# Attention with paired exponentials, bursts of six score pairs, a fold left out and weight loads moved

## The reference, cut to what matters

```python
qkv = jnp.einsum('bsd,de->bse', x, Wqkv)
q, k, v = jnp.split(qkv, 3, axis=-1)
q = _layernorm_scale_only(q, q_ln_scale)
k = _layernorm_scale_only(k, k_ln_scale)
...
scores = jnp.einsum('bshd,bthd->bhst', q / jnp.sqrt(jnp.float32(HEAD_DIM)), k)
scores = jnp.where(causal, NEG_INF, scores)
attn = jax.nn.softmax(scores, axis=-1)
ctx = jnp.einsum('bhst,bthd->bshd', attn, v)
out = jnp.einsum('bsd,de->bse', ctx.reshape(B, S, D_MODEL), out_W)
```

## Time and profile before

| | us |
|---|---|
| median of three runs | 2298.71 |
| lowest and highest | 2298.39, 2300.82 |
| profiled execution, its own time | 2299.94 |
| its span in the profile | 2298.2 |

### The profile page before, as it was taken

How to read it: one execution, slowest core, us unless ns; L and a number is a source line. 1 busy time by engine, 2 the same in 40 slices (tenths; PEclk the granted TensorE clock), 3 DMA queues, 4 the chain that set the end, 5 groups by cost and what they waited for, 6 DMA issues and landing times.

```text
span 2298.2 us, 35041 instructions
## 1 busy us (share of the span) xinstructions
PE 2245.0 (98%) x12270; PEld 1427.9 (62%) x12270; DVE 1698.9 (74%) x1749; ACT 1366.4 (59%) x2821; POOL 302.8 (13%) x366
## 2 busy tenths in 40 slices
PE   9999999999899998999989999899999999999997
PEld 7888854444344443444434444488888888888886
DVE  7777768889798897988979989845655555565554
ACT  4444479999899998999989999611111111101111
POOL 2111122111221112221122211100000000000001
PEclk9999989999999999999999999999999999999999
DMA  7768896657656577556675555831102111110100
GB/s 261 260 239 283 275 247 143 147 132 164 143 135 146 131 158 151 130 141 136 148 158 133 138 120 134 247 108 37 56 19 74 38 37 40 35 55 19 37 19 20
DMA packets 139410, 292.93 MB, mean 127 GB/s; under 512 B 15944, under 2 KB 41032, under 8 KB 127568
## 3 DMA queue, kind: packets, MB, share of 16 engines
q1 hardware_dynamic: 125840, 194.72, 29.6%
q0 software_dynamic: 13104, 95.43, 18.6%
q10 hardware_dynamic: 288, 0.52, 0.1%
HBM read 122.83 MB, written 72.37 MB: 85 GB/s over the span
## 4 chain that ended last, share of the span: by engine, by line
PE 74%; DMA 4%; ACT 4%; DVE 1%; SPq 1%; issue 1%; POOL 0%; DVEq 0%; ACTq 0%; POOLq 0%
PE slot L1555 20%; PE ctx_acc L1145 18%; PE score L1130 18%; PE y L1566 10%; PE slot L1480 3%; ACT probs L1211 3%; PE score_spare L1130 3%; DMA side_odd<-total 2%; DMA side_odd<-probs 1%; PE score L877 1%; DMA queries<-shift 1%; SPq L76 1%; PE slot L1523 1%; POOL probs L1057 0%; PE y L1480 0%
## 5 line engine op out<-in xcount | busy, mean ns | idle before, releaser
L1211 ACT ACTIVATE probs<-score 128x512 f32<-128x512 f32 (+3 forms) x1977 | 987.3, 694 | 69.9 <-DVE total L1273 25.4
L1268 DVE TENSOR_TENSOR total<-total,probs 128x2048 f32<-128x2048 f32 (+3 forms) x440 | 932.2, 2119 | 107.3 <-ACT probs L1211 52.3
L1130 PE MATMUL score<-queries,keys 98*128 98x512 f32 (+3 forms) x1973 | 572.8, 402 | 26.7 <-ACT probs L1211 24.0
L1130 PEld LDWEIGHTS score<-queries,keys 98*128 98x128 f32 x1973 | 346.2, 190 | 366.8 <-ACT probs L1211 287.0
L1631 ACT ACTIVATE hidden<-slot,gate_scale_sb 128x512 f32<-128x512 f32 x128 | 88.4, 690 | 631.6 <-PE slot L1555 628.2
L1145 PE MATMUL ctx_acc<-probs,values 128*32 128x512 f32 (+3 forms) x3584 | 417.2, 564 | 3.8 <-ACT ctx_out L1187 2.0
L1693 DVE SCALAR_TENSOR_TENSOR hidden<-slot,up_scale_sb,hidden 128x512 f32<-128x512 f32 x128 | 96.1, 751 | 253.0 <-ACT hidden L1631 253.0
L1555 PE MATMUL slot<-xt_hi,w_front 128*128 128x512 f32 x600 | 233.6, 389 | 0.0
L1555 PE MATMUL slot<-xt_lo,w_front 128*128 128x512 f32 x600 | 233.5, 389 | 0.0
L1211 ACT ACTIVATE probs<-score_spare 128x512 f32<-128x512 f32 (+3 forms) x327 | 226.6, 693 | 6.2 <-PE score_spare L1130 4.4
L1057 POOL TENSOR_SCALAR_AFFINE_SELECT probs<-probs 128x512 f32<-128x512 f32 x128 | 148.4, 1162 | 495.8 <-ACT probs L1211 495.0
(11 more groups left out here) (171 smaller groups left out, 2530.3 us busy)
## 6 DMA issues: line engine op xcount, KB each, us to landing
side_odd<-probs POOLq DMA_DIRECT2D x40, 1024.0 KB, 7.2
side_even<-probs POOLq DMA_DIRECT2D x32, 1024.0 KB, 7.5
queries<-q_hi SPq DMA_DIRECT2D x64, 256.0 KB
keys<-k_hi SPq DMA_DIRECT2D x64, 256.0 KB
wq_int<-in_wq SPq DMA_DIRECT2D x48, 256.0 KB, 3.3
wq_float<-wq_f SPq DMA_DIRECT2D x48, 256.0 KB, 2.8
side_odd<-total POOLq DMA_DIRECT2D x11, 1024.0 KB, 7.0
x_raw<-in_x_t SPq DMA_DIRECT2D x32, 256.0 KB, 4.5
```

The costliest lines, as they stand in the source:

```text
L1130: pe.matmul(bank(slot)[:, cut(t):], keys[0:ROWS, kb // ST, h, kb % ST * P:(kb % ST + 1) * P], queries[0:ROWS, q_buffer[ch], h, cut(t):], s ...
L1211: act.activation(probs[:, t % PB, h, cut(t):], bank(slot)[:, cut(t):], ACT.Exp).then_inc(exped, 1)
L1268: dve.tensor_tensor(into, into, now, ALU.add).then_inc(added, 1)
```

## The change

Five edits, in `attend` if nothing else is said.

1. The six score banks become one PSUM tensor instead of three (in `build`; `project` uses the same banks under other names).
2. Two successive heads whose banks are neighbours in that tensor (the pair's first slot modulo 7 is 0 to 4) go through one exponential of twice the columns, 1024 in a full step. It waits for both scores and gives both banks back at its end. Pairs that begin in bank 5 or 6 stay two exponentials.
3. Inside a chunk three steps share a burst: six pairs (twelve scores), then three context steps.
4. Chunk 7 is not folded any more (`FOLDED` has chunks 3 to 6). TensorE sums its `total` and its side total with eight matmuls into one bank, behind context step 3 of the next group (for the last group, as before, at the end).
5. In the last chunk of the last group the loads of the inverse sums and of the first weight block stand ahead of the store of chunk 6's sums, and weight blocks 1 to 4 behind it; 5 and 6 stay behind the loop.

```diff
-    FOLD_LAG, SUM_LAG, SIDE_SUM_LAG = 4, 3, 11
+    FOLDED = (3, 4, 5, 6)
+    FOLD_LAG, SUM_LAG, SIDE_SUM_LAG, FOLD_SUM_LAG = 4, 3, 4, 11
...
-        want = 2 * (t + LAG) + 2 if alone else 2 * t + (8, 6)[(place(t) - RUN_FROM) % 2]
+        want = 2 * (t + LAG) + 2 if alone else 2 * t + (10, 8, 6)[(place(t) - RUN_FROM) % 3]
...
-            return spare if b == BANKS - 1 else score[b // 2][:, b % 2, :]
+            return spare if b == BANKS - 1 else score[:, b, :]
...
-            if ch in QUEUED:
+            if ch in FOLDED:
                 pe.wait_ge(folded, 16 * (NF * g + folds_before(ch) + 1))
             else:
                 pe.wait_ge(added, NA * g + adds_before(last[ch] + 1) + A_CREDIT)
...
+                for h in range(HG):
+                    ins = pe.matmul(to[h * HD:(h + 1) * HD, :], ones[:], total[:, ch % 2, h, :], start=True, stop=ch not in QUEUED)
+            if ch in QUEUED:
+                if ch not in FOLDED:
+                    pe.wait_ge(side_added, 16 * (NQ * g + queued_before(last[ch])))
+                for h in range(HG):
+                    ins = pe.matmul(to[h * HD:(h + 1) * HD, :], ones[:], sides[ch % 2][:, h, :], start=ch in FOLDED, stop=True)
...
+                    elif ch == NCH - 1 and at == 8:
+                        sp.wait_ge(inverse_stored, 16 * NG + 16)
+                        wait_scored(NG - 1, key_end[NCH - 1] + 1)
+                        inv_load(sp, dr, keep, 0)
+                        for b in range(2):
+                            sp.wait_ge(keep["wq_stored"][b], 16 * (3 * IC // 2) + 16)
+                        front(0)
+                    elif ch == NCH - 1 and at == 26:
+                        for j in range(1, 5):
+                            front(j)
...
-                    elif g and t == FOLD_LAG:
-                        fold(g - 1, NCH - 1)
...
-                        for h in (2 * p, 2 * p + 1):
+                        slot = slot_of(g, HG * t + 2 * p)
+                        if slot % BANKS < BANKS - 2:
+                            act.wait_ge(scored, slot + 2 + Q_CREDIT)
+                            act.activation(probs[:, t % PB, 2 * p:2 * p + 2, cut(t):],
+                                           score[:, slot % BANKS:slot % BANKS + 2, cut(t):], ACT.Exp).then_inc(exped, 2)
+                        for h in (2 * p, 2 * p + 1) if slot % BANKS >= BANKS - 2 else ():
```

More of the change, by code:

```diff
@@ L232, in project @@
         whole = keep["whole"]
-        turn = [keep["score"][2][:, i, :] for i in range(2)]
-        acc = [keep["score"][i // 2][:, i % 2, :] for i in range(ACCS)]
+        turn = [keep["score"][:, ACCS + i, :] for i in range(2)]
+        acc = [keep["score"][:, i, :] for i in range(ACCS)]
         norms = [c.enter_context(nc.psum_tensor(f"norms_{n}", [P, 512], F32)) for n in "qk"]
@@ L757, in folds_before @@
     def folds_before(ch):
-        return sum(x < ch for x in QUEUED)
+        return sum(x < ch for x in FOLDED)
     adds = [t for t in range(NS) if t not in queued]
@@ L780, in attend @@
         g, ch = divmod(gc, NCH)
-        sum_behind[divmod(NS * g + last[ch] + (SIDE_SUM_LAG if ch in QUEUED else SUM_LAG), NS)] = (g, ch)
+        sum_behind[divmod(NS * g + last[ch] + (FOLD_SUM_LAG if ch in FOLDED else SIDE_SUM_LAG if ch in QUEUED else SUM_LAG), NS)] = (g, ch)
     sum_behind = dict(sorted(sum_behind.items()))
@@ L874, in sum_total @@
                 pe.wait_ge(added, NA * g + adds_before(last[ch] + 1) + A_CREDIT)
-            data = sides[ch % 2][:] if ch in QUEUED else total[:, ch % 2, :, :]
-            for h in range(HG):
-                ins = pe.matmul(to[h * HD:(h + 1) * HD, :], ones[:], data[:, h, :], start=True, stop=True)
+                for h in range(HG):
[5 more added lines that the diff above has]
+                    ins = pe.matmul(to[h * HD:(h + 1) * HD, :], ones[:], sides[ch % 2][:, h, :], start=ch in FOLDED, stop=True)
             return ins
         def sum_last(pe):
[L882 to L888, removed]
+            sum_total(pe, NG - 1, NCH - 1, spare).then_inc(totaled, 1)
         def wait_total_free(dve, g, ch):
@@ L894, in wait_total_free @@
                 return
-            if before in QUEUED:
+            if before in FOLDED:
                 dve.wait_ge(folded, 16 * (NF * gb + folds_before(before) + 1))
@@ L975, in load_kv, with front @@
                 value_load(sp, dr, value_rows(j), g, j, v_in[j])
+            def front(j):
+                wait_scored(NG - 1, key_end[j] + 1)
+                weight_load(sp, dr, keep, keep["w_front"][:, j * ST:(j + 1) * ST, :], j)
             stored(sp, NCH)
@@ L1092, in pool_attention @@
                         add_aside(g, t)
-                    if ch and place(t) == FOLD_LAG and ch - 1 in QUEUED:
+                    if ch and place(t) == FOLD_LAG and ch - 1 in FOLDED:
                         fold(g, ch - 1)
-                    elif g and t == FOLD_LAG:
-                        fold(g - 1, NCH - 1)
         def pe_attention(pe, general):
@@ L1106, in pe_attention @@
                         pe.wait_ge(g_read, NU * g + u + 1)
-                        pe.matmul(score[u % 2][:, 0, :], queries[0:ROWS, 0, h, qt * P:(qt + 1) * P],
+                        pe.matmul(score[:, 2 * (u % 2), :], queries[0:ROWS, 0, h, qt * P:(qt + 1) * P],
                                   keys[0:ROWS, kc, h, :], start=True, stop=True).then_inc(g_scored, 1)
@@ L1907, in build @@
             early_psum = ExitStack()
-            keep["score"] = [early_psum.enter_context(nc.psum_tensor(f"score{i}", [P, 2, CH], F32)) for i in range(3)]
+            keep["score"] = early_psum.enter_context(nc.psum_tensor("score", [P, 6, CH], F32))
             project(nc, io, dr, keep)
```

20 lines of the change are left out of this document (7 added, 13 removed).

## The result

| | median, us | range, us | profiled run, us | its span, us |
|---|---|---|---|---|
| before | 2298.55 | 2298.1 to 2300.82 | 2299.94 | 2298.2 |
| after | 2369.98 | 2368.22 to 2375.92 | 2375.92 | 2373.8 |

The ratio is 1.0306, 95% interval 1.0292 to 1.032: 71.4 us slower. The forecast was 2351 us, so the direction held and the time lies within the range, but the sum was 19 us short.

A forecast was written before the change was run, and what follows sets the result against it. The prediction took TensorE to set the pace, with ScalarE 0.09 us from being the bound. Its terms, 87 - 27 - 8 = +52 us, gave 2351 us against the median, range 2315 to 2392.

The forecast's parts named there:

- What bounds the kernel: In attention TensorE sets the pace, ScalarE is 0.09 us from being the bound; three context blocks exceed seven banks.
- The long burst: Chunks 3 to 7: three steps cost 6.64 us against 5.86, since banks return late; 112 bursts, +87 us.
- the seven ways in which a burst's pairs can lie: First three pairs of a burst, by which is single: score 11 starts at 3.32 to 3.80 us, mean 3.59.
- The joined exponential: ScalarE's exponential of 1024 columns: between 0.86 and 0.955 us, taken at 0.91 by the slope.
- The rival that had it much quicker: 1024 columns in about 0.5 us let bursts run unstalled: 2245 us; break-even at 0.69 us; chance 0.11.
- The border: Between groups, chunk 7's fold goes and a TensorE sum replaces it: -27 us, from -15 to -32.
- The rival that the border only changes its wait: Between groups the new sum is waited for as long as the fold, nothing gained: 2378 us; chance 0.05.
- The end: Last chunk: moved weight loads leave 2 MB less beside four side sums: -8 us, between 0 and -10.
- the step that failed: Side copies by DMA in ordinary chunks: given no cost; side sums were weighed only in the last chunk.
- the two repairs: Chunk 7's fold dropped between groups, -27 us, and weight loads moved in the last chunk, -8 us.
- The rival that had half clock in each of the 20 chunks: TensorE in chunks 3 to 7: one half-clock stretch per chunk, +101 us, 2452 us; chance 0.05.

The follow-up runs named there:

- three_single: Changed kernel with every exponential single (512 columns), bursts of twelve scores and three context steps kept: 2338.01 us, 1.0163 of before.
- half_exp: Changed kernel, but from chunk 2 on (first group from chunk 4) each whole exponential takes only 256 of its 512 columns: 2260.74 us, 0.9823 of before.
- fold_back: Changed kernel with the fold of chunk 7's total by DMA put back: 2393.45 us, 1.0399 of before.
- loads_back: Changed kernel with inverses and all weight blocks again loaded behind the store of chunk 6's sums: 2376.56 us, 1.0334 of before.
- side_later: Changed kernel, but in chunks 4 and 6 VectorE adds step 5 in place of the DMA side copy: 2360.23 us, 1.0256 of before.
- repairs: Changed kernel with bursts of eight scores and two context steps and no joined exponentials; border and weight loads stay changed: 2272.68 us, 0.9882 of before.

## Why the prediction was right in its mechanism and 19 us short

**What bounds the kernel.** Right. TensorE set the pace, ScalarE was close behind, and three context steps in a row were more than seven banks cover. The range was wider than its own bounds at the lower end: all of them at once give 2319, not 2315. Nothing hangs on it here.

**The long burst.** Predicted +87, measured about +90. In the timeline of TensorE the seven ways in which a burst's pairs can lie take 6.47, 6.72, 6.89 and 6.97 us, where the prediction had 6.37, 6.61, 6.80 and 6.85: each 0.09 to 0.12 more. The row after a held score tells most of it: from 1218.30 to the context steps at 1218.72 it is 0.42 us, where I had taken 0.34, the time of a last score that was not held; `three_single` has 0.43 at the same place (602.33 to 602.76). So a held score cost about 0.08 us more before the context steps than one that was not held; what that time is, no run shows. The four classes weigh in at 6.74, +0.88 a burst. The whole chunks 3 to 7, timed by the copies of their contexts where nothing else disturbs them, grew in the first group by 2.3, 3.3, 4.2, 5.8 and 6.9 us, 22.5 in 28 bursts: 0.80 each. Four such groups give 90 us. Why a chunk grew by less than its bursts is not shown, so that 90 came so near to 87 is in part luck: the bursts were longer than forecast, and something beside them made up for it.

**The joined exponential.** Taken at 0.91, measured at 0.905. By the Trainium skill, "ScalarE: Activation LUTs", section "What ACT_TABLE_LOAD costs", the estimate was 0.95; the trace gives less, as it did at 512 columns. The rival that had it much quicker needed under 0.69 and falls. `half_exp` shows that its arithmetic was right: with short exponentials the burst takes 5.67 us, where it gave 5.69.

**The border.** Predicted -27, measured -21 by `fold_back`, -26 by the copies of the contexts at the three borders. The timeline of ScalarE has chunk 0's and chunk 2's copies of the second group, beside the last two of the earlier trace rows, at:

```profile
633.48 0.63 ACT L1192 ACTIVATE ctx_out<-ctx_acc 128x512 f32<-128x512 f32 x1
...
674.32 0.60 ACT L1192 ACTIVATE ctx_out<-ctx_acc 128x512 f32<-128x512 f32 x1
```

40.84 us, where 49.28 stood. The rival that the border only changes its wait falls with it, although the new wait is there: VectorE's 12.2 us in three, up to 4.1, where I had allowed 0.6. It is paid by VectorE, whose work has room there: the longest wait of TensorE's scores for ScalarE is 1.0 us.

**The end.** Predicted -8, measured -6 by `loads_back`, not sure to be more than nothing. The ScalarE group at the end of attention had waited for the side sums' DMA for 7.5 us; in the changed kernel all the 6.6 us of idle time before its joined exponentials there are waits for TensorE. In the groups between 1480 and 1552 us:

```profile
L1215 ACT ACTIVATE probs<-score 128x1024 f32<-128x1024 f32 x42 | 41.5, 1048 | 6.6 <-PE score L1135 6.6
```

**The side copies: the step that failed.** The prediction weighed the side sums only in the last chunk. In the ordinary chunks it costed them at nothing, and named no work that hides them. There the copy of step 5 stands behind the fold on Pool's queue; changed timing brought the two within 0.57 us of each other, and in later groups, above all in chunks 4 and 6, TensorE stood and then ran at half clock. `side_later` puts this at about 11.5 us (1.0306 - 1.0256 = 0.0050; the medians differ by 9.8). `three_single` has such stalls too: its bursts of 6.36 us make 112 x 0.50 = 56 of the 65 us that it lies over `repairs`, and some 9 are left. That fits the stalls, but no run takes the copy out of that kernel. The other reason why it ran over is that the two repairs together gave 27 us, where its range was reckoned from 35.

With it the sum is 90 - 26 - 6 + 11.5 = 69.5, against 71.4 measured. By these figures, of the 19 us short, some 11 are the step that failed, 3 the longer bursts, 3 the repairs that were a little smaller, and 2 are left over. The runs alone split it otherwise. The repairs are 27 by `repairs`, as 21 and 6 are one by one, and from `repairs` to `side_later` the bursts with their joined exponentials are 1.0256 - 0.9882 = 0.0374, 86 us. Then 86 - 27 + 11.5 = 70.5: 8 of the 19 lie in the repairs and none in the bursts. Both ways have the same 11 for the side copies; how the rest divides is known only to some 5 us.

**The clock.** The rival that had half clock in each of the 20 chunks falls: from 400 to 600 us, with TensorE standing for some 0.4 to 0.5 us in most bursts of twelve, the granted clock was 1.00. Inside chunks it fell in a few bursts behind a side copy, as after the 1.03 and 0.41 us at 820.88 and 822.77. A burst with much the same stands (0.95, 0.42, 0.18 and 0.18 us, begun at 1390.42) passed at full clock, so what decides it is open. The rule of the Trainium skill, "TensorE: Matmul & The Clock Gate", section "A second HAM failure mode: psum-queue depth-cycling", by which this rival would have been the outcome, is thus not borne out here for stands of 0.4 to 0.5 us a burst.

## What to carry to other kernels

Before a burst on one engine is made longer, count the buffers: score k of a burst waits for the reader of score k minus the number of banks, and if that reader is done only after the score's turn has come, the burst is held. Here that wait cost more than the saved switches brought. Joining two operations to save a fixed cost holds both their buffers to the end, so join those whose buffers nobody wants next and leave the head of each burst single (34 us here, by one pair in four). And when a change shifts the timing, look at every DMA that is issued right behind another one, in the steady part too, not only where the profile shows a wait now.

## What the runs showed of the hardware

- An exponential over two PSUM banks, 1024 columns, took 0.905 us from one to the next against 2 x 0.477 for two single ones: joining saves 0.05 us. In this kernel both banks come back only at its end.
- After a score that had to wait, the context step started 0.42 us behind it, against 0.34 after one that had not.
- One copy, issued 0.57 us behind another transfer of the same size, landed after 10.92 us, where the median of such transfers was 7.2.
- TensorE kept full clock from 400 to 600 us through stands of 0.4 to 0.5 us in most bursts of 6.5 to 7 us. Half clock (822.50 to 829.30) followed stands of 1.03 and 0.41 us in one burst, but stands of 0.95 and 0.42 us in another (1392.34 and 1394.23) left the clock at 1.00.
